# SSM, self-attention and cross-attention in one kernel: B-C products in pairs, the last SSM group in two halves, low halves by turns

## What is computed

```python
# part 1: five SSM layers and one self-attention layer, on layernorm(x)
def ssm_layer(x, Wi, cw, cb, Wo, g, b):
    proj = x @ Wi                                   # 256 -> 512 + 64 + 64
    xs, Bm, Cm = proj[..., :512], proj[..., 512:576], proj[..., 576:]
    u = silu(causal_conv(xs, cw) + cb)              # 4 taps along the tokens
    # h[t] = -0.5 * h[t-1] + u[t] (x) B[t];  y[t] = h[t] . C[t]
    return layer_norm(y @ Wo + x, g, b)
def attn_layer(x, wq, wk, wv, wo, g, b):            # 16 heads of 64, causal
    return layer_norm(softmax(mask(q @ k.T / 8)) @ v @ wo + x, g, b)
x = x + L0_attn(layernorm(x))
# part 2: cross-attention to ctx_1024, 16 heads of 16
x = x + L0_xattn(layernorm(x), ctx_1024)
# then: 8 experts, 2 chosen for each token; a second attention; a second
# cross-attention; a product with int8 rounding. The change leaves them alone.
```

## Time and profile before

| | us |
|---|---|
| median of 3 runs (lowest, highest) | 1241.9 (1240.51, 1242.79) |
| the profiled execution | 1241.41 |
| its span, first to last instruction | 1239.7 |
| SSM stage, with its first projections | 27 to 374 |
| self-attention | 374 to 695 |
| cross-attention | 695 to 851 |
| experts | 851 to 1116 |

### The profile page before, as it was taken

How to read it: one execution, slowest core, us unless ns; L and a number is a source line. 1 busy time by engine, 2 the same in 40 slices (tenths; PEclk the granted TensorE clock), 3 DMA queues, 4 the chain that set the end, 5 groups by cost and what they waited for, 6 DMA issues and landing times.

```text
span 1239.7 us, 22821 instructions
## 1 busy us (share of the span) xinstructions
PE 1156.2 (93%) x7635; PEld 927.0 (75%) x7635; DVE 799.7 (65%) x1827; ACT 708.2 (57%) x2030; POOL 714.4 (58%) x776
## 2 busy tenths in 40 slices
PE   3999999999969999999989799988999999998996
PEld 3888888888857888888877677767666666667775
DVE  6778888888843667666676588876332333324796
ACT  2868777787843655655555488881223444225873
POOL 3599898989760224343353677761457556542664
PEclk9999999999988999999999899999999999999999
DMA  4300000010102000000010124601522222222001
GB/s 146 128 18 31 18 7 25 15 30 18 17 1 69 1 2 1 2 1 2 2 51 19 60 78 154 256 19 35 154 45 43 44 47 47 44 34 68 1 27 43
DMA packets 40228, 55.92 MB, mean 45 GB/s; under 512 B 8416, under 2 KB 35040, under 8 KB 38592
## 3 DMA queue, kind: packets, MB, share of 16 engines
q1 hardware_dynamic: 31392, 44.38, 10.7%
q0 software_dynamic: 8736, 10.25, 5.1%
HBM read 42.88 MB, written 11.74 MB: 44 GB/s over the span
## 4 chain that ended last, share of the span: by engine, by line
PE 45%; issue 7%; ACT 7%; DVE 7%; POOL 3%; DMA 1%; POOLq 0%; ACTq 0%; DVEq 0%
PE bank L1602 11%; PE bank L1619 5%; ACT x_prob L1256 4%; PE bank L44 4%; PE bank L45 3%; PE bank L46 3%; PE bank L711 2%; PE bank L739 2%; PE bank L722 2%; PE bank L1350 1%; PE bank L1611 1%; PE bank L1366 1%; PE bank L604 1%; PE bank L1296 1%; PE bank L2092 1%
## 5 line engine op out<-in xcount | busy, mean ns | idle before, releaser
L440 DVE SCALAR_TENSOR_TENSOR ssm_conv<-bank,conv_w,ssm_conv 128x508 f32<-128x508 f32 (+2 forms) x240 | 160.8, 734 | 25.9 <-ACT ssm_conv L356 25.9
L777 ACT ACTIVATE a_prob<-a_prob,a_neg_max 128x128 f32<-128x128 f32 x256 | 99.7, 391 | 117.8 <-DVE a_neg_max L823 117.8
L1602 PE MATMUL bank<-expert_raw,x_kept_next_t 128*128 x312 | 146.7, 593 | 1.2 <-ACT x_kept_next_t L1682 1.2
L883 POOL TENSOR_TENSOR a_prob<-a_prob,a_inv 128x512 f32<-128x512 f32 x64 | 66.6, 1041 | 138.7 <-DVE a_inv L828 138.7
L552 POOL TENSOR_TENSOR ssm_u_lo<-ssm_conv,ssm_u_hi 128x512 fp32r<-128x512 f32 x80 | 101.4, 1289 | 26.4 <-ACT ssm_conv L366 26.3
L1544 POOL DMA_INDIRECT x_rows<-e_y,e_index x39 | 62.8, 1611 | 75.8 <-ACT e_y L1710 72.1
L1256 ACT ACTIVATE x_prob<-bank,x_neg_max 128x128 f32<-128x128 f32 x256 | 89.9, 402 | 11.6 <-DVE x_neg_max L1233 11.5
L1826 DVE COPY e_h_t<-bank 128x512 f32<-128x512 f32 x39 | 27.0, 692 | 105.3 <-PE bank L1611 105.3
L44 PE MATMUL bank<-w_out_hi,ssm_u_hi 128*128 128x256 f32 x320 | 91.9, 287 | 1.1 <-POOL ssm_u_lo L552 1.1
L1143 POOL TENSOR_TENSOR x_prob<-x_prob,x_inv 128x512 f32<-128x512 f32 x64 | 67.0, 1052 | 42.6 <-DVE x_inv L1237 42.1
L46 PE MATMUL bank<-w_out_hi,ssm_u_lo 128*128 128x256 f32 x320 | 90.5, 283 | 0.0
(11 more groups left out here) (340 smaller groups left out, 3367.8 us busy)
## 6 DMA issues: line engine op xcount, KB each, us to landing
expert_raw<-in_experts_laid SPq DMA_DIRECT2D x8, 1536.0 KB, 8.9
attn_raw<-in_attn_w_laid SPq DMA_DIRECT2D x1, 4096.0 KB, 12.4
w_in_raw<-in_L_attn_in_proj_w SPq DMA_DIRECT2D x5, 640.0 KB, 5.9
w_out_raw<-in_L_attn_out_proj_w SPq DMA_DIRECT2D x5, 512.0 KB, 4.0
x_res<-in_x SPq DMA_DIRECT2D x4, 512.0 KB, 5.5
x_res<-in_x SPq DMA_DIRECT2D x1, 2048.0 KB, 8.5
x_context<-in_ctx_t_laid SPq DMA_DIRECT2D x8, 256.0 KB, 3.7
z_rows<-x_kept_next_z SPq DMA_DIRECT2D x8, 256.0 KB, 2.2
```

Of the source, the lines that this page charges most:

```text
L440: op = dve.scalar_tensor_tensor(out=acc, in0=xs, scalar=conv_w[:, c, TAPS - 1 - back:TAPS - back], in1=acc, op0=ALU.mult, op1=ALU.add)
L777: e = act.activation(prob[:, m % 4, i, :], prob[:, m % 4, i, :], ACT.Exp, bias=neg_max[:, m % 4, i:i + 1], accum_out=total[:, m % 4, i:i + 1])
L883: pool.tensor_tensor(prob[:, t % 4, :, :], prob[:, t % 4, :, :], inv[:, t % 4, :].unsqueeze(2).broadcast_to([P, 4, P]), ALU.mult).then_inc ...
L1602: mm = pe.matmul(bank[:, :], rows_t[:, t % 2, k, :], W[:, bass.ds(at + (column + k * FFN), FFN)], start=(k == 0), stop=(k == KD - 1))
```

## The change

1. The four B-C products become two pairs. `b_t` and `c_t` keep two sequences in partitions 0 to 63 and two in 64 to 127, so ACT makes four copies of 256 columns instead of two of 512. The pairs go to two banks, `BC` and `TR` (in the last group `BC` and `XS(0)`), and DVE's decay product is made in two parts. `TR` is also the bank of the transposes: PE waits for `tr_low` ahead of the B-C products, and for `mix_ready` ahead of the first transposes instead of behind them.
2. POOL's split of an attention weight stands behind `invert`, and the four splits of u stand together.
3. The last group of the last layer is normalised in two halves: statistics and inversion by halves, the first half by ACT and POOL as before, the second by DVE alone; the second half is turned first, into `TR`, the first into `XS(2)`. PE issues 20 idle products before, 4 behind.
4. Self-attention's low half has two buffers in turns (the second in `act_t_lo`). Units 30 and 31 are split one tick earlier. The 9 idle products behind unit 30's product are gone.
5. v is cleared by a DMA of zeros from memory on SP instead of POOL's memset. What is due before 2000 (three maxima of sequence 0) is issued behind tick 71, ahead of tick 72.

```diff
 def mix_tokens(layer, g, first=False, last=False):
-    for s in range(GS):
-        mm = pe.matmul(BC[:, s * P:(s + 1) * P], b_t[:, g % 2, s * P:(s + 1) * P],
-                       c_t[:, g % 2, s * P:(s + 1) * P], start=True, stop=True)
-    mm.then_inc(g_ready, 1)
+    if not (first and g < 2) and not last:
+        pe.wait_ge(tr_low, n * 2 - 2)
+    if last:
+        pe.wait_ge(conv_done, n * KI + KI)
+    for s in range(GS // 2):
+        for half, bank in enumerate(product_banks(last)):
+            rows = slice(half * STATE, (half + 1) * STATE)
+            mm = pe.matmul(bank[:, s * P:(s + 1) * P], b_t[rows, g % 2, s * P:(s + 1) * P],
+                           c_t[rows, g % 2, s * P:(s + 1) * P], start=True, stop=True,
+                           tile_position=(half * STATE, 0))
...
+    pe.wait_ge(mix_ready, n + 1)
     if before:
         turn(*before, 0)
-    pe.wait_ge(mix_ready, n + 1)
 # PE, behind the loop
-for h in range(2):
-    turn(LAST, GROUPS - 1, h)
+keep_at_work(pe, mem, 1, 20)
+for h, ready, count in ((1, res_ready, n * 2 + 6), (0, act_ready, n * 2 + 1)):
+    pe.wait_ge(ready, count)
...
+    tr.then_inc(tr_ready, 1)
+keep_at_work(pe, mem, 1, 4)
 # DVE, behind the loop: the second half of the last group
+dve.wait_ge(shift_ready, n + 2)
+for s in range(2):
+    dve.tensor_scalar(res[:, 1, s, :], res[:, 1, s, :], mv[:, i, 0:1], rstd[:, i:i + 1],
+                      ALU.subtract, ALU.mult).then_inc(res_ready, 1)
+dve.tensor_tensor(res[:, 1, :, :], res[:, 1, :, :], ln_g..., ALU.mult)
+dve.tensor_tensor(ACTV[:, SEQS - 2:SEQS, :], res[:, 1, :, :], ln_b..., ALU.add)
 # POOL, behind the loop
+pool.tensor_tensor(rstd[:, 0:2], rstd[:, 0:2], neghalf[:, 0:2], ALU.pow)
+pool.tensor_tensor(shift[:, 0:2], neg_mean[:, 0:2], rstd[:, 0:2], ALU.mult).then_inc(shift_ready, 1)
+pool.wait_ge(var_ready, n + 2)
+pool.tensor_tensor(rstd[:, 2:4], rstd[:, 2:4], neghalf[:, 0:2], ALU.pow).then_inc(shift_ready, 1)
+finish(LAST, GROUPS - 1, 0)
 # self-attention
+def split_at(m):
+    early = m in (TICKS + SPLIT - 5, TICKS + SPLIT - 3)
+    unit = behind(m, SPLIT - 1 if early else SPLIT)
+    return unit if early or not unit or unit[0] < TICKS // 2 - 2 else None
-    if U > 0:
-        dve.wait_ge(y_ready, U)
-    dve.tensor_tensor(o_t_lo[:, :, :], OT(U)..., o_t_hi..., ALU.subtract)
+    if U > 1:
+        dve.wait_ge(y_ready, U - 1)
+    dve.tensor_tensor(o_t_lows[U % 2], OT(U)..., o_t_hi..., ALU.subtract)
-    if U == TICKS // 2 - 2:
-        keep_at_work(pe, mem, 0, 9)
 # cross-attention
-LEAD = {72: 0}
+LEAD = {71: 2000}
-    pool.memset(v[:, :, :, :, :], 0.0).then_inc(v_cleared, 1)
+    sp.dma_start(v..., io["noughts"]).then_inc(v_cleared, 16)   # behind job_ready, as the memset
```

More of the change, by code:

```diff
@@ L163, in split_w_in, with keep_at_work @@
     pool.tensor_tensor(chunks(lo), chunks(raw), chunks(hi).bitcast(F32), ALU.subtract).then_inc(names["w_in_split"], 1)
+def keep_at_work(pe, mem, bank, products):
+    ident = mem["ident"]
+    for _ in range(products):
+        pe.matmul(mem["psum"][bank][:, 0:P], ident[:, :], ident[:, :], start=True, stop=True)
 def stage_ssm(nc, ctx, io, mem):
@@ L495, in layer_steps @@
                         convolve(*ahead, 0)
-                    decayed(layer, g)
+                    decayed(layer, g, last and g == GROUPS - 1)
                     if ahead:
@@ L501, in layer_steps @@
                         turned_low(*before, 0)
-                    norm(layer, g)
+                    if last and g == GROUPS - 1:
+                        last_norm()
+                    else:
+                        norm(layer, g)
                     if before:
@@ L564, in layer_steps @@
                         invert(*before)
+                    if not last:
+                        split_attention_weight(layer, g)
                     for h in range(2):
@@ L597 @@
 OCT = KW // 2
-def keep_at_work(pe, mem, bank, products):
-    ident = mem["ident"]
-    for _ in range(products):
-        pe.matmul(mem["psum"][bank][:, 0:P], ident[:, :], ident[:, :], start=True, stop=True)
 def stage_self_attention(nc, ctx, io, mem):
```

126 lines of the change are left out of this document (92 added, 34 removed).

## The result

The changed kernel takes 1224.6 us (median of 4 runs, 1223.57 to 1225.16) against 1241.9 (4 runs, 1240.51 to 1242.79): ratio 0.9861, 95% interval 0.9844 to 0.9878, so 17.3 us faster. The prediction said 1223.6, between 1217 and 1230. Its sum held, its terms did not: the pairs gave 1.9 us less than forecast, the end of self-attention 1.4 more, and the term of the clock, 1.2 more in the two profiled executions, depends on where the low stretches of TensorE's clock fall. The profiled execution of the changed kernel is the fastest of its four (1223.57); its mean granted clock is 0.994, that of the other three 0.991.

A forecast was written before the change was run, and what follows sets the result against it. The prediction took TensorE (PE) to pace the SSM stage and self-attention, whose ends are chains of short operations. Savings of 9.8 + 2.4 + 1.0 + 1.1 + 3.5 = 17.8 us from 1241.4 gave 1223.6, range 1217 to 1230.

The forecast's parts named there:

- Pairs: SSM stage: B-C products issued in pairs save 0.54 us in each of groups 1 to 18; 9.8, bounds 0 and 10.8.
- So pairs take half, 0.54 us: SSM stage: a set of four B-C products takes 1.08 us; as pairs it takes half, judged by self-attention's scores.
- Last group in halves: End of the SSM stage: normalising by halves ends DVE's last low half 2.4 us earlier, bounds 1.5 and 4.0.
- The collision: Last SSM group: DVE's z are held behind POOL's two operations, so product and sum end at 368.5 instead of 366.9.
- PE kept at work: End of the SSM stage: idle products may keep TensorE's clock from falling; 1.0 us, bounds 0 and 2.4.
- v by DMA: Self-attention: without POOL's memset the mask on DVE is not stretched from 0.68 to 1.83; 1.1 us, at most 1.8.
- End of self-attention: Units 30 and 31 split a tick earlier, cross-attention's maxima ahead of the last z: 3.5 us.
- POOL's 2.8 and ACT's 4.9: End of self-attention: gain 2.8 us by POOL's path to the first share-out, 4.9 by ACT's exponentials; 3.5 taken.
- Attention split: SSM stage: moved behind the inversion it fills POOL's 1.27 us of idling; worth 0 itself, gives the 9.8 slack.
- the pairs run side by side: Against the rival that SSM's pairs run one after the other: the 9.8 lost, 1233.4 us, chance 0.07.
- no engine took over: Against the rival that POOL or DVE needs 65 us per SSM layer: 6 us lost, 1229.6, chance 0.10.
- the ends paid: Against the rival that the SSM and self-attention ends don't pay: 2 of 6.9 us remain, 1228.5, chance 0.20.

The follow-up runs named there:

- the kernel with the lead moved back: Changed kernel with cross-attention's first maxima on DVE again behind self-attention's last z, low halves still early, idle products still out: 1225.2 us, ratio 0.986.

## Why the prediction held, term by term

**Pairs: 9.8 forecast, 7.9 measured in the groups, 7.5 with what the copies cost.** The step that failed is "So pairs take half, 0.54 us". Half of the set's moving time (0.88, four times 0.22) is saved; the 0.21 of going to 64 rows is not. The row of the scores in the earlier trace rows could not show this, since it has the same share. With 0.65 instead of 0.54 the step 18 x 0.43 gives 7.7. That PE paces the groups stands: doubling the sets made the steps from set to set 0.44 longer, all but the first, which kept its 15.63, and those at the layers' ends, which grew by 0.3 to 0.6. ACT's four copies were put at nothing, inside ACT's idle time. That holds in the groups, but ahead of the first set PE waits for them: 0.35 more, where the forecast let group 0 gain 0.2. DVE's two decay products and both new waits cost nothing that the marks show.

**Last group in halves: 2.4 forecast, 2.5 measured, of which 0.7 is the clock.** The forecast took the last transposes at 0.6 us; before they took 1.12 (at 0.50), so its 2.4 held a part of the clock's gain unsaid. With the clock low in both kernels the halves give 1.8. The collision came as reckoned: sum at 362.15 in this trace is 368.4 on the old clock (6.25 earlier there), forecast 368.5. The order of the turns gave away 0.6.

**PE kept at work: 1.0 forecast, 2.2 in this pair of executions.** With the 0.7 above it is 2.9, more than its upper bound of 2.4. The choice between the bounds could not be read from the old trace, and over many executions the runs settle no more than 0 to 2.5.

**v by DMA: 1.1 forecast, 1.2, and 0.6 of clock behind it.** The forecast left out what PE's wait does to the clock.

**End of self-attention: 3.5 forecast, 4.9 measured.** Its times were right: maxima at 677.15, which is 689.9 on the old clock (12.75 earlier there), share-out 681.75, 694.5, both as forecast. The step that failed is the last, the 3.5 taken between POOL's 2.8 and ACT's 4.9. ACT paces the stage behind, and the marks of the kernel with the lead moved back show it.

**Attention split: 0 by itself.** Right that it makes room; wrong that room was only just lacking. 3.5 us hang on it, at the layers' ends.

The sum of the measured terms is 7.9 + 2.5 + 2.2 + 1.8 + 4.9 = 19.3; the start's -1.6 (1.3 of clock, 0.35 of copies) and small shifts of the clock behind bring it to 17.9 in span, and 17.3 between the medians. So the total was right partly by luck: 1.9 too much in the pairs against 1.4, 1.2 and 0.7 too little elsewhere, and then 1.4 at the start and in the clock, which no term held. None of the rivals came about: the pairs run side by side, no engine took over (POOL would have, at the layers' ends, without the split moved), the ends paid, and the decay product's wait shows no gap ahead of the first transposes. Of the signs that were named, POOL no longer idles between the inversion and `finish` between groups 8 and 9, a set takes 0.65 and a group 15.99 where 0.6 and 15.9 were named; self-attention's first product is 8.7 us earlier (365.15 against 373.88), not 12, for the pairs gave less and the start came later.

## What to carry to other kernels

- A short group of products has a share that does not shrink with its work. Before a set is halved, double it, or find rows of two lengths: the slope is what the change saves.
- A layer's mean need of an engine hides the group in which its extra work falls. Compare the busiest group with the new period, not the mean.
- With differences under 2 us, read the shift of equal operations at marks along the program, place by place. Here the totals agreed with forecasts whose terms were wrong, and hid terms that were right.

## What the runs showed of the hardware

Going from full products to products over 64 rows and back cost TensorE 0.35 us in the group with pairs; 0.21 on top of the products' own time shows in the set, paired or not.

The clock's low stretches are not a fixed property of a kernel. The mean granted clock of the changed kernel was 0.994 in one and 0.991 in three of its executions. The start of full rate lay between 30.3 and 33.4 us in the fourteen traces, with the same code ahead of it. The 3.4 us at 0.50 near 1110 to 1133 came in eight of the thirteen traces other than that of the kernel before, and was absent in five; it moves what follows by some 1.7 us. Part of this comes back: in four of these five the next low stretch, from 1206 to 1215 on, lasts 6.8 to 6.9 us, where it lasts 3.4 in the eight. PE was idle for 3.2 us ahead of 362.2 in the changed kernel and the clock stayed full, while it was 0.50 from 362.0 to 365.4 in the kernel with self-attention's end as before, which is the same up to there.

DVE and POOL hold each other up in both directions: a z with one tensor input in SBUF took 1.35 and 1.42 us instead of 0.40 beside POOL's product and sum, which kept their 1.27 and 1.26; and when DVE's product came first, POOL's sum took 1.66 instead of 1.26. The Trainium skill (SBUF — State Buffer, Who interferes with whom) names `tensor_scalar` among the operations that can take the shared pair of ports, and the z is one; by that the trace agrees. It also says that two SBUF inputs do not collide with an operation that only writes. The memset held the operation on two columns until 642.78 in the earlier trace rows; that one is a `tensor_scalar` and no two-input operation, and whether the mask would have been held by itself was not tried.
